# First attention of a two-layer tower: two heads of a step run two products apart, with a count for each fill

## The reference

```python
Q, K, V = (heads(z @ W + b) for W, b in ((Wq, bq), (Wk, bk), (Wv, bv)))   # 8 heads of 16
qk = einsum('bhnd,bhmd->bhnm', Q, K)
nf_q = abs(Q - mean(Q)).sum(-1) / (sqrt(var(Q) + EPS) + EPS)
omega = (q2[..., None] + k2[..., None, :] - 2 * qk) / (exp(-nf_q) + 1)
out = softmax(qk / sqrt(16) - omega) @ V @ Wo + bo
...
q = x @ Wq + bq                        # product-key memory: queries against keys
s1, s2 = einsum('bhc,hnc->bhn', q1, keys[:, 0]), einsum('bhc,hnc->bhn', q2, keys[:, 1])
```

## Time and profile before

| | |
|---|---|
| median of 3 runs | 1126.18 us (1122.7 to 1128.15) |
| profiled execution, its own time | 1123.27 us |
| its span, first to last instruction | 1121.3 us |
| granted TensorE clock, mean over the span | 0.941 of full |
| first row product of step 0 | 47.75 us |
| step 64, when only column products are left | 226.07 us |

### The profile page before, as it was taken

How to read it: one execution, slowest core, us unless ns; L and a number is a source line. 1 busy time by engine, 2 the same in 40 slices (tenths; PEclk the granted TensorE clock), 3 DMA queues, 4 the chain that set the end, 5 groups by cost and what they waited for, 6 DMA issues and landing times.

```text
span 1121.3 us, 21964 instructions
## 1 busy us (share of the span) xinstructions
PE 960.1 (86%) x8152; PEld 687.9 (61%) x8152; DVE 819.2 (73%) x2594; ACT 500.5 (45%) x1042; POOL 399.8 (36%) x335
## 2 busy tenths in 40 slices
PE   3587887996988888889888877899999988889997
PEld 3454444453878777778787875545545545467775
DVE  5666767568999999999999953466665565362887
ACT  1124555563344434434334332566565654344332
POOL 4664652000444453343333340455444454300000
PEclk9588999997899999999999897899999998989999
DMA  4101300000000000000000012000000000000000
GB/s 108 31 1 30 141 1 1 1 1 1 2 2 1 1 2 1 1 1 2 1 2 2 2 39 75 1 1 1 1 1 1 1 1 1 1 1 1 10 9 19
DMA packets 6720, 14.12 MB, mean 13 GB/s; under 512 B 1885, under 2 KB 4766, under 8 KB 6046
## 3 DMA queue, kind: packets, MB, share of 16 engines
q1 hardware_dynamic: 5598, 10.70, 2.9%
q0 software_dynamic: 1024, 2.10, 0.7%
HBM read 11.74 MB, written 1.05 MB: 11 GB/s over the span
## 4 chain that ended last, share of the span: by engine, by line
PE 53%; DVE 28%; issue 7%; ACT 6%; POOL 4%; DVEq 1%; POOLq 0%; DMA 0%; SPq 0%; ACTq 0%
PE quad L1859 5%; PE bank L1854 5%; PE quad L1740 4%; PE bank L1713 4%; DVE i L1134 4%; DVE w_v L1217 4%; PE bank L1765 4%; PE bank L1516 4%; PE bank L1751 4%; PE quad L1702 3%; PE bank L1629 3%; PE bank L1607 3%; PE bank L1535 2%; DVE one_u L1223 2%; ACT a_e L841 2%
## 5 line engine op out<-in xcount | busy, mean ns | idle before, releaser
L565 POOL TENSOR_TENSOR vals<-relu_in,g_sb 128x512 f32<-128x512 f32 x80 | 125.5, 1608 | 157.4 <-DVE one_u L1223 130.0
L600 POOL TENSOR_TENSOR a_e<-a_e,a_rrec 128x1024 f32<-128x1024 f32 x64 | 121.2, 1893 | 149.3 <-DVE a_rrec L1318 149.3
L1629 PE MATMUL bank<-xnT,wd 128*128 128x128 f32 x1024 | 141.1, 295 | 33.9 <-ACT relu_in L717 33.8
L1629 PEld LDWEIGHTS bank<-xnT,wd 128*128 128x128 f32 x1024 | 130.2, 205 | 45.8 <-ACT relu_in L717 41.8
L1713 PE MATMUL bank<-wu,vals 128*128 128x128 f32 x1024 | 119.5, 278 | 4.8 <-issue 4.8
L1713 PEld LDWEIGHTS bank<-wu,vals 128*128 128x128 f32 x1024 | 118.2, 195 | 4.9 <-issue 4.9
L841 ACT ACTIVATE a_e<-quad,a_negmax 128x512 f32<-128x512 f32 x128 | 86.8, 683 | 38.2 <-DVE a_negmax L1311 34.4
L1516 PE MATMUL bank<-a_kT,a_qT 32*128 32x512 f32 x344 | 83.7, 451 | 21.6 <-DVE a_q_aug L1026 13.4
L671 ACT ACTIVATE a_eT<-quad 128x512 f32<-128x512 f32 x128 | 73.9, 599 | 57.6 <-PE quad L1520 57.1
L1311 DVE TENSOR_REDUCE a_negmax<-quad 128x2 f32<-128x1024 f32 x64 | 77.9, 1217 | 22.3 <-PE quad L1740 21.6
L717 ACT ACTIVATE relu_in<-bank 128x512 f32<-128x512 f32 x128 | 73.6, 593 | 40.9 <-PE bank L1629 40.4
(11 more groups left out here) (229 smaller groups left out, 1903.3 us busy)
## 6 DMA issues: line engine op xcount, KB each, us to landing
wd<-in_pk_down SPq DMA_DIRECT2D x1, 2048.0 KB, 7.8
wu<-in_pk_up SPq DMA_DIRECT2D x1, 2048.0 KB, 12.3
wu<-in_moe_w SPq DMA_DIRECT2D x2, 1024.0 KB, 5.8
out<-h SPq DMA_DIRECT2D x4, 256.0 KB, 2.3
wd<-in_num_rows SPq DMA_DIRECT2D x1, 512.0 KB
a_eT<-in_pk_wqT SPq DMA_DIRECT2D x1, 512.0 KB, 6.4
a_eT<-in_pk_keys SPq DMA_DIRECT2D x1, 512.0 KB, 7.9
wu<-in_event_table,idx_e POOLq DMA_INDIRECT x16, 2.5
```

The costliest lines, as they stand in the source:

```text
L565: nc.gpsimd.tensor_tensor(*weigh_args(t, c, k, g_sb[:, slot, :])).then_inc(vals_pool, 1)
L600: nc.gpsimd.tensor_tensor(e1[:, g % 4], e1[:, g % 4], rrec1[:, g % 4].unsqueeze(2).to_broadcast([P, 2, S]), ALU.mult).then_inc(a1.nr, 1)
L1629: last = mm(bank[g % 2][:, q * P:(q + 1) * P], wd[:, IG * g + q, :], xnT_tile(t), start=True, stop=True)
```

## The change

- In `logits0` the two heads no longer go side by side. Head 0 of step `g + 1` makes its first two products beside head 1's last two of step `g`. Two lone products of head 0 stand ahead of the loop.
- Each fill has its own count, up and down: `a0.rows` and `a0.cols` count heads, `rowmax0` and `exp0` wait for their own head, and TensorE waits for the bank of each fill (`fill - 2`) at that fill's first product.
- `BANK7_0` is laid out anew: most duties from sequence 1 on sit on odd steps. Calls in the loops move with it (`copy_outT` to the start of a step, `nf0` and `exp_nf` to step 11, `factors0` to 12, `ln_stats` apart from `embed_tokens`).
- `key_weights` moves ahead of the first queries, into banks 5, 0, 1 and 2, with its copies and subtractions; the first queries go through banks 3 and 4; the loop starts when all of it is read.

```diff
@@ -51,7 +51,7 @@
-    KEY_BANKS = (3, 4, 5, 3)
+    KEY_BANKS = (5, 0, 1, 2)
@@ -290,16 +290,16 @@
-             12: ("k", 3), 13: ("xnT", 2), 14: ("qkv", (2, 0)), 15: ("q", 2)},
-            {0: ("qkv", (2, 1)), 1: ("q2", 1), 2: ("qkv", (2, 2)), 5: ("q", 3), 7: ("xnT", 3), 8: ("k", 4), 9: ("q2", 2),
-             10: ("back", 0), 11: ("qkv", (3, 0)), 12: ("k", 5), 13: ("qkv", (3, 1)), 14: ("qkv", (3, 2)), 15: ("q", 4)},
-            {1: ("q2", 3), 2: ("back", 1), 4: ("fwd", 0), 5: ("q", 5), 6: ("out", 0), 8: ("k", 6), 9: ("q2", 4),
-             10: ("back", 2), 12: ("k", 7), 15: ("q", 6)},
-            {1: ("q2", 5), 2: ("back", 3), 3: ("tile", 0), 4: ("fwd", 1), 5: ("q", 7), 6: ("out", 1), 7: ("score", (0, 0)),
-             8: ("score", (0, 1)), 9: ("q2", 6), 10: ("back", 4), 11: ("tile", 1), 12: ("score", (1, 0)),
-             13: ("score", (1, 1))},
-            {1: ("q2", 7), 2: ("back", 5), 4: ("fwd", 2), 6: ("out", 2), 7: ("tile", 2), 8: ("score", (2, 0)),
-             9: ("score", (2, 1)), 10: ("back", 6), 12: ("uvp", 0), 15: ("back", 7)},
+             12: ("xnT", 2), 13: ("qkv", (2, 0)), 14: ("q", 2), 15: ("k", 3)},
+            {0: ("qkv", (2, 1)), 1: ("q2", 1), 2: ("qkv", (2, 2)), 5: ("q", 3), 6: ("xnT", 3), 9: ("q2", 2), 10: ("k", 4),
+             11: ("back", 0), 12: ("qkv", (3, 0)), 13: ("qkv", (3, 1)), 14: ("q", 4), 15: ("k", 5)},
+            {0: ("qkv", (3, 2)), 1: ("q2", 3), 3: ("back", 1), 5: ("q", 5), 7: ("fwd", 0), 8: ("out", 0), 9: ("q2", 4),
+             10: ("k", 6), 11: ("back", 2), 14: ("q", 6), 15: ("k", 7)},
+            {1: ("q2", 5), 3: ("back", 3), 4: ("tile", 0), 5: ("q", 7), 6: ("score", (0, 0)), 7: ("fwd", 1), 8: ("out", 1),
+             9: ("q2", 6), 10: ("score", (0, 1)), 11: ("back", 4), 12: ("tile", 1), 13: ("score", (1, 0)),
+             15: ("score", (1, 1))},
+            {1: ("q2", 7), 3: ("back", 5), 5: ("fwd", 2), 7: ("out", 2), 8: ("tile", 2), 9: ("score", (2, 0)),
+             10: ("score", (2, 1)), 11: ("back", 6), 13: ("uvp", 0), 15: ("back", 7)},
@@ -664,10 +664,9 @@
             def exp0(s, r):
...
-                if r == 0:
-                    act.wait_ge(a0.cols, s + 1)
-                    if pair >= 3:
-                        act.wait_ge(a0.pv, (pair - 3) // 2 * TPB + c + 1)
+                act.wait_ge(a0.cols, 2 * s + r + 1)
+                if r == 0 and pair >= 3:
+                    act.wait_ge(a0.pv, (pair - 3) // 2 * TPB + c + 1)
@@ -696,9 +695,11 @@
+            for n in range(4):
+                key_weights(n)
...
-                query_hi(g, bank[1 - g])
+                query_hi(g, bank[3 + g])
@@ -756,10 +757,10 @@
             for g in range(END0):
+                if outT_at(g) is not None:
+                    copy_outT(outT_at(g))
...
-                if g in (2, 4, 6, 8):
-                    key_weights(g // 2 - 1)
@@ -781,13 +782,11 @@
-                if outT_at(g) is not None:
-                    copy_outT(outT_at(g))
...
-                    if u == 12:
+                    if u == 11:
                         exp_nf(b + 1)
@@ -1020,11 +1019,17 @@
             def rowmax0(g):
...
-                dve.wait_ge(a0.rows, g + 1)
...
+                    dve.wait_ge(a0.rows, 2 * g + r + 1)
...
+            def key_bias_lo(n):
+                cols = slice(n % 2 * 512, (n % 2 + 1) * 512)
+                dve.wait_ge(kw_sb, n + 1)
+                V.tensor_tensor(keyb[32:33, cols], bank[KEY_BANKS[n]][0:1, :], keyb[0:1, cols].bitcast(F32),
+                                ALU.subtract).then_inc(kb_lo, 1)
@@ -1065,18 +1070,20 @@
+            dve.wait_ge(ld_pk, 48)
+            V.tensor_copy(bqb_s, bq_s[:].unsqueeze(2).to_broadcast([P, H, P])).then_inc(bq_b, 1)
...
+            for n in (2, 3):
+                key_bias_lo(n)
...
-                query_lo(g, bank[1 - g])
-            dve.wait_ge(ld_pk, 48)
-            V.tensor_copy(bqb_s, bq_s[:].unsqueeze(2).to_broadcast([P, H, P])).then_inc(bq_b, 1)
+                query_lo(g, bank[3 + g])
@@ -1092,31 +1099,26 @@
-                if g in (6, 8):
-                    n = g // 2 - 1
-                    dve.wait_ge(kw_sb, n + 1)
-                    cols = slice(n % 2 * 512, (n % 2 + 1) * 512)
-                    V.tensor_tensor(keyb[32:33, cols], bank[KEY_BANKS[n]][0:1, :], keyb[0:1, cols].bitcast(F32),
-                                    ALU.subtract).then_inc(kb_lo, 1)
...
+                    if u == 11:
+                        nf0(b + 1)
                     if u == 12:
-                        nf0(b + 1)
-                    if u == 13:
                         factors0(b + 1)
-                    n = 2 if g == 6 else 3
-                    embed_tokens(n)
+                    embed_tokens(2 if g == 6 else 3)
+                if g in (8, STEPS0 + 4):
+                    n = 2 if g == 8 else 3
                     ln_stats(lnB, n * TPB, TPB)
-                if g in (12, STEPS0 + 5):
-                    n = 2 if g == 12 else 3
+                if g in (11, STEPS0 + 5):
+                    n = 2 if g == 11 else 3
...
-                if g == 2 * STEPS0 + 8:
+                if g == 2 * STEPS0 + 10:
                     ln_stats(lnC, 0, TPB)
@@ -1455,8 +1457,6 @@
-                if n == 3:
-                    pe.wait_ge(kw_sb, 1)
@@ -1490,39 +1490,53 @@
-            def logits0(g):
-                rows_now, cols_now = g < ALL0, 0 <= g - SHIFT < ALL0
-                if rows_now:
-                    pair, j = g // TPB, g % TPB
-                    gr, first = pair // 2, pair % 2 * 2
-                    if j == 0 and pair % 2 == 0:
+            def row_product(g, r, n):
+                pair, j = g // TPB, g % TPB
+                gr, tile = pair // 2, pair % 2 * 2 + r
+                fill = 2 * g + r
+                if n == 0:
+                    if j == 0 and pair % 2 == 0 and r == 0:
...
-                    if g:
-                        pe.wait_ge(a0.mx, 2 * g - 1)
-                if cols_now:
-                    s = g - SHIFT
-                    pair2, c = s // TPB, s % TPB
-                    gr2, first2 = pair2 // 2, pair2 % 2 * 2
-                    if c == 0 and pair2 % 2 == 0:
-                        pe.wait_ge(a0.q2_lo, gr2 + 1)
-                    if s:
-                        pe.wait_ge(a0.ex, 2 * s - 1)
-                for n, (qp, kp) in enumerate(((0, 0), (0, 1), (1, 0), (1, 1))):
-                    for r in range(2):
-                        if rows_now:
-                            part = slice((first + r) * AUG, (first + r + 1) * AUG)
-                            row = mm(bank[S1_BANKS[(2 * g + r) % 3]], qT0[part, qp, gr % 2, j * P:(j + 1) * P],
-                                     kT0[part, kp, gr % 4, :], start=(n == 0), stop=(n == 3))
-                        if cols_now:
-                            part = slice((first2 + r) * AUG, (first2 + r + 1) * AUG)
-                            col = mm(bank[S2_BANKS[(2 * s + r) % 3]], kT0[part, kp, gr2 % 4, c * P:(c + 1) * P],
-                                     q2T0[part, qp, gr2 % 2, :], start=(n == 0), stop=(n == 3))
-                if rows_now:
-                    row.then_inc(a0.rows, 1)
-                if cols_now:
-                    col.then_inc(a0.cols, 1)
+                    if fill >= 3:
+                        pe.wait_ge(a0.mx, fill - 2)
+                part = slice(tile * AUG, (tile + 1) * AUG)
+                made = mm(bank[S1_BANKS[fill % 3]], qT0[part, n // 2, gr % 2, j * P:(j + 1) * P],
+                          kT0[part, n % 2, gr % 4, :], start=(n == 0), stop=(n == 3))
+                if n == 3:
+                    made.then_inc(a0.rows, 1)
...
+            def col_product(s, r, n):
+                pair, c = s // TPB, s % TPB
+                gr, tile = pair // 2, pair % 2 * 2 + r
+                fill = 2 * s + r
+                if n == 0:
+                    if c == 0 and pair % 2 == 0 and r == 0:
+                        pe.wait_ge(a0.q2_lo, gr + 1)
+                    if fill >= 3:
+                        pe.wait_ge(a0.ex, fill - 2)
+                part = slice(tile * AUG, (tile + 1) * AUG)
+                made = mm(bank[S2_BANKS[fill % 3]], kT0[part, n % 2, gr % 4, c * P:(c + 1) * P],
+                          q2T0[part, n // 2, gr % 2, :], start=(n == 0), stop=(n == 3))
+                if n == 3:
+                    made.then_inc(a0.cols, 1)
...
+            def head_product(g, r, n):
+                if 0 <= g < ALL0:
+                    row_product(g, r, n)
+                if 0 <= g - SHIFT < ALL0:
+                    col_product(g - SHIFT, r, n)
...
+            def logits0(g):
+                for n in range(2):
+                    head_product(g, 0, 2 + n)
+                    head_product(g, 1, n)
+                for n in range(2):
+                    head_product(g + 1, 0, n)
+                    head_product(g, 1, 2 + n)
@@ -1590,9 +1604,14 @@
+            pe.wait_ge(ld_pk, 48)
+            for n in range(4):
+                key_weights(n)
```

(12 more changed lines are left out.)

## The result

The changed kernel takes 1131.61 us (median of 13 runs, 1128.28 to 1134.93) against 1122.28 for the kernel before (13 runs on the same chips): ratio 1.0074, 95% interval 1.0051 to 1.0097. It is slower by about 8 us, where 7.6 less were forecast. Its profiled execution has a span of 1132.9 us, 11.6 more than before; it took 1134.79 us, 3.2 above the median, so differences between the two profiles are somewhat larger than that of the medians.

The account below looks back on a forecast made before the run. No engine was taken as full until the tail (TensorE); chains bound the early stages, row-maximum waits the later. Terms -7.9 + 1.5 - 1.5 - 1.4 + 1.0 + 0.7 = -7.6 us gave 1117 us, range 1105 to 1125.

Parts of the forecast that it names:

- The tail, +0.7: Stretch after step 63: 0.7 us more, for one odd-step duty there that ends in a ScalarE copy.
- TensorE is full there: Tail: TensorE busy 35.59 of 36.13 us, so shorter waits can't shorten it.
- Steps 4 to 12, -9.0: Step 4 to VectorE's `nf0` of sequence 1: 18.0 us instead of 26.97, from less VectorE work and idle time.
- 12.3 and 18.0: Forecast lengths in us: steps 0 to 3 (from 14.37), then step 4 to `nf0(1)` (from 26.97).
- the second rival: Early stretch stays slow because row products alone may keep the clock low: no change, about 1125 us, chance 0.23.
- The front: Before the first row product: key weights placed there make it end 2.9 us later, bounds 1.4 and 5.2.
- ScalarE's wait: Steps 23 to tail: second half-step waits 0.6 to 0.7 us for an exp, 15 odd-step places, 10.5 us given back.
- The gain on the other side: Steps 23 to 63: TensorE's waits for row maxima and new queries down from 10.4 us to about 3.
- To step 23, +1.5: From `scale_queries(1)` to step 23: 1.5 us more, as `ln_stats` a step later delays GpSimd; bounds 0 and 2.5.
- Counts: 0: All 64 steps: four counted fills instead of two taken as free; bounds 0 and 5.1 us.
- the 3.4: Cost in us of 128 added counts, estimated by the Trainium skill's some 26 ns each; gain then 4.1.

Follow-up runs that it names:

- residual first: Changed kernel with VectorE's step 71 (residual of sequence 2) executed ahead of the key retrieval block instead of behind it: 1125.08 us, ratio 1.0014.
- old last row: Table's line for steps 64 to 79 put back as before; in the changed kernel with nothing else edited: 1124.05 us, ratio 1.0002.
- Front alone: Kernel before, with only the key weights made ahead of the first queries instead of in steps 1, 3, 5 and 7: 1129.94 us, ratio 1.0054.
- the kernel without the front: Changed kernel with key weights back in steps 1, 3, 5 and 7 and the table's line for steps 64 to 79 as before: 1120.96 us, ratio 1.0006.
- ballast: Changed kernel with the key weights' 32 products made again in steps 1, 3, 5 and 7, read by nobody: 1130.07 us, ratio 1.0065.
- exps together: Changed kernel with ScalarE's two exps of a step ahead of the shared-bank copy: 1122.95 us, 0.9984; same edit in the kernel without the front: 1108.56 us, 0.9860.
- the table alone: Kernel before with the new table's first four rows and the calls that move, its last row as before, products in lockstep: 1115.00 us, ratio 0.9927.
- lockstep with the counts: Kernel before with the new table's first four rows, last row as before, and a count for each fill, heads side by side: 1112.98 us, ratio 0.9906.

## Why the prediction was wrong

By the events, -7.6 was forecast for the end and 11.6 measured. Of these 19.2 us, 5.1 are missing by `scale_queries(1)` (-2.8 for -7.9), 4.9 from there to step 25 (+6.0 for +1.1), 1.8 to step 65 (+0.3 for -1.5), 6.7 in the tail (+7.4 for +0.7) and 0.7 behind it, which is below what that part varies by. (I reckoned from 1126.18, the median of three runs; by thirteen it is 1122.28.)

**The tail, +0.7, was the largest error: it was +7.4.** The step that failed is the sentence that TensorE is full there, so that only its own work counts. `out(2)` went from step 70 to 71, one line of the table, and I did not look at what VectorE's program has between steps 70 and 71: the term had nothing for it, and it cost TensorE 6.07 at once. Undoing it gave 0.6% to 1.0% in each of four pairs of kernels (residual first, which moves nothing else; the old last row in three).

**Steps 4 to 12, -9.0, came out short because TensorE's clock fell.** I sized that stretch by VectorE's work. From the first product to `nf0(1)` I had 12.3 and 18.0, it took 36.33 (15.9 in steps 0 to 3, as far as 65.88, and 20.4 behind them), with TensorE busy for 35.72 at 0.50: TensorE set the pace, not VectorE. That is the mechanism of the second rival, and more than it: the key weights had been work, but work that kept the clock up. Front alone shows it (+5.3 at `scale_queries(1)`), the kernel without the front shows it (36.55, so that taking them out gained 0.2), and ballast shows it from the other side. How much of the 6.0 missing in this stretch a full clock would give is not shown: ballast gave 2.0 (`nf0(1)` at 84.45 from a first product at 50.06), with its own 32 products in the way. The front itself was nearly right, +2.2 for +2.9.

**ScalarE's wait was right in mechanism and size, and wrong in its reach.** I put 0.7 on 11 places in steps 32 to 63, 7.7 us; taking the wait away gained 7.0 from step 33 to 65 (80.1 against 73.1), where the trace has 11 such waits. The 0.7 does not show as idle time (0.2 to 0.3), which I had said it would: the rest is three idle quarters of the array and a second start of the block, 1.90 against 1.14. But column products run from step 12, and I counted places only from 23. Steps 12 to 25 had the same wait, three times (at 100.73, 103.72 and 106.22), and with the exps together step 25 comes 3.7 sooner (128.72 against 132.38). That is most of the 4.9 missing there, though three places at 0.7 are only 2.1 of it.

**The gain on the other side** is there: TensorE's waits for maxima did fall, and with the exps together steps 25 to 65 take 93.4 us (222.14 less 128.72). In the change they take 101.8, before 101.5: ScalarE's order gives back all of it, where I had all but 1.5. But most of that gain isn't the staggered order's, to which I gave it: in the kernels without the front the table alone takes these steps from 101.5 to 96.8, the counts to 95.4, and the staggered order with the exps together to 93.2. In lockstep with the counts TensorE's products already stand still for maxima only 1.7 us from 115 to 230, without the counts 7.2.

**To step 23, +1.5**, was about right for the table and short for the whole. GpSimd's norm came 3.4 later than the 112.18 in the earlier trace rows, 24.9 behind `scale_queries(1)` instead of 18.8, and ScalarE stands on its keys longer:

```profile
115.59 1.04 POOL L478 TENSOR_TENSOR rstd<-veps,mhalf 128x4 f32<-128x4 f32 x1 [11.35 <-DVE veps L923]
...
122.11 0.63 ACT L639 ACTIVATE a_k<-a_k_aug 128x512 f32<-128x512 f32 x1 [5.85 <-POOL a_k_aug L494]
...
123.79 0.79 PE L1521 MATMUL quad<-a_q2T,a_kT 32*128 32x512 f32 x1 [2.84 <-ACT a_eT L670]
```

TensorE waits 2.84 for the exp behind that, where it waited 3.7 in the earlier trace rows, and the same 2.8 is left in the kernel with exps together. With the table's new first four rows alone the norm is 20.7 behind `scale_queries(1)`, 2.0 more than before; the staggered order adds the rest, and the exps together take it back to 22.0. What `ln_stats` one step later does by itself was not tried.

**Counts: 0 was right**; the lockstep kernel with them is no slower. (By the 3.4 the gain would have been 4.2, not 4.1.) The range (1105 to 1125) ended where one loss, the second rival's, would have brought the time; it held no case in which two came together, and none for the tail.

## What to carry to other kernels

When an order moves an operation by one step, look up on every engine what its program does between the old step and the new one; a block of other work there is the price, however full the engine you look at is. Before a finer-grained schedule is judged, put the instructions that release its buffers ahead of those that can wait: here that and the table's old last row turned a loss of 0.7% into a gain of 1.2%. Work taken out of a stretch may be what keeps TensorE's clock up there, so its removal has to be priced at the lower clock: here 32 products fewer gained 0.2 us.

## What the hardware showed that I had not expected

Four products in four quarters of the array are as fast as two (sixteen took 1.14, from 148.31 to 149.45; eight in the tail took 1.12, from 250.13 to 251.25), but they start in order: one that waits holds those behind it. The Trainium skill says so ("TensorE: Matmul & The Clock Gate", section "The mechanism": matmuls start and end in program order), and the row at 153.91 agrees, alone for 0.68 us. The busy time counts such a lone product as fully as four. With the exps together PE's 981.2 us become 977.3, so this is only a part of the 21 us over the 960.1 of before. 15 of them arise up to step 25, where part of the work ran at a lower granted clock than before; what the clock's share is, no run separates.

From the first row product to `nf0(1)` 102 of TensorE's 144 products were row products, two quarters of the array at a time (24 more were projections), and the granted clock stood at 0.50 for the whole 36 us, though TensorE was busy for 98% of them. With a bank of key weights behind every second step it was 0.97 to 1.00 between 60 and 75 us.
